# A decoder layer on one core: the weight products of its prologue chunk by chunk, and the first rows loaded beside them

## What is computed

```
x_norm = (x - mu) / sqrt(var + EPS) * gamma + beta
q = x_norm @ qkv[:, :KEY]
k = x_norm @ qkv[:, KEY:2 * KEY]
v = x_norm @ qkv[:, 2 * KEY:]
scores = einsum('bsk,btk->bst', q, k) * scale     # causal mask, softmax over t
out = attn @ v
out = out @ o_proj
return out + residual
```

## Time and profile before

| | |
|---|---|
| times of three runs | 1488.83, 1490.62, 1490.15 us; median 1490.15 |
| the profiled execution's own time | 1488.81 us |
| its span | 1487.0 us |
| TensorE busy | 1440.3 us, 97% of the span |
| VectorE, ScalarE, GpSimd busy | 71%, 44%, 39% |
| self-attention stage, from the trace | 0 to about 385 us |
| its prologue, until the bodies' first matmul | 0 to 40.99 us |

### The profile page before, as it was taken

One profiled execution on the slowest core, in us unless ns is written; L12 is line 12 of the kernel. 1 busy time (PEld: TensorE's weight loads), 2 busy tenths in 40 slices (PEclk: granted clock), 3 DMA queues, 4 the chain that ended last, 5 costly groups with the idle time before them and its releaser, 6 DMA issues. The chain is left out here.

```text
span 1487.0 us, 33650 instructions
## 1 busy us (share of the span) xinstructions
PE 1440.3 (97%) x13322; PEld 1123.5 (76%) x13322; DVE 1055.3 (71%) x2021; ACT 656.9 (44%) x865; POOL 579.2 (39%) x510
## 2 busy tenths in 40 slices
PE   7899999999899999999999999999999996899898
PEld 3688888887788888888888888888888885455343
DVE  2866565564477777877777778777787777677898
ACT  1333333333343343433433433334333332789996
POOL 0000000000144544555445545454545453753576
PEclk9999999999999999999999999999999998899999
DMA  6023333321511212112111121121111210439895
GB/s 219 29 79 103 103 103 102 102 76 52 184 41 42 73 45 72 39 45 72 45 47 64 45 72 39 45 72 45 56 55 45 72 46 24 107 113 327 274 348 200
DMA packets 80743, 138.59 MB, mean 93 GB/s; under 512 B 5218, under 2 KB 52834, under 8 KB 78898
## 3 DMA queue, kind: packets, MB, share of 16 engines
q1 hardware_dynamic: 80690, 137.87, 28.4%
HBM read 93.82 MB, written 44.04 MB: 93 GB/s over the span
## 5 line engine op out<-in xcount | busy, mean ns | idle before, releaser
L737 POOL TENSOR_TENSOR xa_psum<-xa_pr 125x448 f32<-125x448 f32 x126 | 153.9, 1221 | 236.3 <-DVE xa_pr L883 236.3
L883 DVE TENSOR_SCALAR xa_pr<-xa_pr,xa_keep 125x448 f32<-125x448 f32 x384 | 151.0, 450 | 108.3 <-ACT xa_pr L783 107.0
L783 ACT ACTIVATE xa_pr<-xa_bSC 125x1344 f32<-125x1344 f32 x128 | 165.6, 1293 | 138.3 <-PE xa_bSC L989 132.3
L764 ACT ACTIVATE xa_kf<-xa_bKV,xa_bk 128x376 f32<-128x376 f32 x128 | 73.6, 575 | 184.9 <-PE xa_bKV L913 184.9
L740 POOL TENSOR_TENSOR xa_psum<-xa_psum,xa_pr 125x448 f32<-125x448 f32 x126 | 147.0, 1167 | 12.1 <-POOL xa_psum L737 4.4
L913 PE MATMUL xa_bKV<-left_xn,wA 128*128 128x376 f32 x768 | 149.9, 344 | 0.0
L913 PE MATMUL xa_bKV<-xa_cx,wA 128*128 128x376 f32 x768 | 149.3, 343 | 0.0
L770 ACT COPY xa_v<-xa_bKV 125x512 f32<-125x512 f32 x96 | 56.2, 585 | 206.2 <-PE xa_bKV L924 201.1
L924 PE MATMUL xa_bKV<-wZ,left_xn 128*125 128x512 f32 x576 | 141.9, 394 | 1.7 <-POOL xa_ones L713 1.7
L924 PE MATMUL xa_bKV<-wZ,xa_cx 128*125 128x512 f32 x576 | 141.1, 393 | 0.0
L913 PEld LDWEIGHTS xa_bKV<-left_xn,wA 128*128 128x128 f32 x768 | 130.0, 188 | 8.9 <-issue 5.3
(11 more groups left out here) (193 smaller groups left out, 2508.8 us busy)
## 6 DMA issues: line engine op xcount, KB each, us to landing
wraw<-in_ctxT SPq DMA_DIRECT2D x32, 752.0 KB, 4.8
ff_hr<-h_scratch SPq DMA_DIRECT2D x28, 512.0 KB, 6.5
wraw<-in_w SPq DMA_DIRECT2D x8, 1024.0 KB, 7.7
sa_raw<-in_x SPq DMA_DIRECT2D x8, 896.0 KB, 5.9
x_scratch<-left_qraw SPq DMA_DIRECT2D x8, 896.0 KB, 5.1
xa_qf<-q_scratch SPq DMA_DIRECT2D x32, 224.0 KB, 4.9
xa_x<-x_scratch SPq DMA_DIRECT2D x32, 224.0 KB, 4.7
x_scratch<-xa_x SPq DMA_DIRECT2D x32, 224.0 KB, 2.3
```

The lines of the kernel that those rows point to most:

```text
L737: nc.gpsimd.tensor_tensor(psum01[:], third(h, 0), third(h, 1), ALU.add).then_inc(p01_ok, 1)
L783: nc.scalar.activation(pr[h][:], bSC[0:TW, :, 0:TC * S], ACT.Exp, scale=XSCALE).then_inc(exp_ok, 1)
L883: nc.vector.tensor_scalar(third(h, t), third(h, t), EM50, bound, ALU.max, ALU.min).then_inc(pr_ok, 1)
```

## The change

wqT and wkT are loaded chunk by chunk (eight loads of 256 KB, in pairs, each pair with a semaphore of its own). Products 0 to 3 are worked on together: for each chunk, the four matmuls into four different banks (`bM[0]`, `bM[1]`, `bS`, `bP`). So all four end in the last chunk. Products 4 to 7 go as before, into `bM[0]` and `bM[1]`, with `turned(0)` behind product 4 where it was ahead of product 7. Behind the eight loads SP loads the rows of group 0 into `x1`, which is the buffer `qraw`, and `statistics(0)` and `normalise(0)` read them there, ahead of every `product_low`. xwq, which needs the same buffer, is loaded once those rows are normalised. The rows of group 0 are loaded into `xt[0]` as well, as before, for the residual sum; VectorE waits for this load there.

```diff
+        bG = bM + [bS, bP] + bM + bM
-            for h in range(2):
+            for c in range(C):
                 for k, w in enumerate((wqT, wkT)):
-                    sp.dma_start(raw[k][:, 2 * h:2 * h + 2, :], w[:, 2 * h:2 * h + 2, :]).then_inc(w_in[h], 16)
+                    sp.dma_start(raw[k][:, c, :], w[:, c, :]).then_inc(w_in[c], 16)
+            sp.dma_start(x1, x_v[0]).then_inc(x0_in, 16)
             for k, w in enumerate((wvT, wo)):
-                sp.dma_start(raw[2 + k][:], w).then_inc(w_in[2 + k], 16)
+                sp.dma_start(raw[2 + k][:], w).then_inc(w_in[C + k], 16)
             for t, v in ((gam, gamma), (bet, beta), (bq, xbq)):
                 sp.dma_start(t[:], v).then_inc(small_in, 16)
-            sp.dma_start(qraw[:], xwq).then_inc(w_in[4], 16)
+            sp.wait_ge(xhat_ok, 4)
+            sp.dma_start(qraw[:], xwq).then_inc(w_in[C + 2], 16)
             sp.wait_ge(prod_done, 4)
...
-                nc.scalar.copy(w[0][:, k % 4, :], bM[k % 2][:, 0:D]).then_inc(prod_hi, 1)
-
-            for k in range(7):
-                product_high(k)
-            act.wait_ge(small_in, 48)
+                nc.scalar.copy(w[0][:, k % 4, :], bG[k][:, 0:D]).then_inc(prod_hi, 1)
...
+            for k in range(5):
+                product_high(k)
+            act.wait_ge(small_in, 48)
             turned(0)
-            product_high(7)
+            for k in range(5, 8):
+                product_high(k)
...
-                nc.vector.tensor_tensor(w[1][:, k % 4, :], bM[k % 2][:, 0:D], w[0][:, k % 4, :].bitcast(F32),
+                nc.vector.tensor_tensor(w[1][:, k % 4, :], bG[k][:, 0:D], w[0][:, k % 4, :].bitcast(F32),
...
             def statistics(g, par):
-                dve.wait_ge(x_in[par], 8 * (g - par) + 16)
+                rows = x1 if first(g) else xt[par]
+                if first(g):
+                    dve.wait_ge(x0_in, 16)
+                else:
+                    dve.wait_ge(x_in[par], 8 * (g - par) + 16)
...
                 dve.wait_ge(rh_ok, g + 1)
+                if first(g):
+                    dve.wait_ge(x_in[0], 16)
...
+            statistics(0, 0)
+            normalise(0, 0)
             for k in range(5):
                 product_low(k)
-            statistics(0, 0)
-            product_low(5)
-            normalise(0, 0)
-            product_low(6)
             split(0)
-            product_low(7)
-            dve.wait_ge(w_in[4], 16)
+            for k in range(5, 8):
+                product_low(k)
+            dve.wait_ge(w_in[C + 2], 16)
...
-            for k in range(8):
-                if k == 7:
+            for c in range(C):
+                pe.wait_ge(w_in[c], 32)
+                for k in range(4):
+                    mm = nc.tensor.matmul(bG[k][:, 0:D], raw[0][:, c, k * P:(k + 1) * P], raw[1][:, c, :], start=c == 0, stop=c == C - 1)
+                    if c == C - 1:
+                        mm.then_inc(prod_done, 1)
+            pe.wait_ge(w_in[C], 16)
+            pe.wait_ge(w_in[C + 1], 16)
+            for k in range(4, 8):
+                pe.wait_ge(prod_lo, k - 3 if k < 6 else k - 1)
+                for c in range(C):
+                    mm = nc.tensor.matmul(bG[k][:, 0:D], raw[2][:, c, (k - 4) * P:(k - 3) * P], raw[3][:, c, :], start=c == 0, stop=c == C - 1)
+                mm.then_inc(prod_done, 1)
+                if k == 4:
                     pe.wait_ge(const_ok, 2)
                     turned(0)
-                if k == 4:
-                    pe.wait_ge(w_in[2], 16)
-                    pe.wait_ge(w_in[3], 16)
-                a, b = (raw[0], raw[1]) if k < 4 else (raw[2], raw[3])
-                wait(pe, prod_lo, k - 1)
-                for c in range(C):
-                    if k == 0 and c % 2 == 0:
-                        pe.wait_ge(w_in[c // 2], 32)
-                    mm = nc.tensor.matmul(bM[k % 2][:, 0:D], a[:, c, (k % 4) * P:(k % 4 + 1) * P], b[:, c, :],
-                                          start=c == 0, stop=c == C - 1)
-                mm.then_inc(prod_done, 1)
```

More of the change, by code:

```diff
@@ L134, in self_attention @@
         bW = bP[:].bitcast(BF16)
+        bG = bM + [bS, bP] + bM + bM
         flat = wraw[:].rearrange("p c d -> p (c d)")
-        w_in, small_in = [n.sem(f"w_in{i}") for i in range(5)], n.sem("small_in")
-        x_in = [n.sem(f"x_in{p}") for p in range(2)]
+        w_in, small_in = [n.sem(f"w_in{i}") for i in range(C + 3)], n.sem("small_in")
+        x_in, x0_in = [n.sem(f"x_in{p}") for p in range(2)], n.sem("x0_in")
         zero_ok, const_ok = n.sem("zero_ok"), n.sem("const_ok")
@@ L331, in product_low @@
                 w = wA if k < 4 else wZ
-                nc.vector.tensor_tensor(w[1][:, k % 4, :], bM[k % 2][:, 0:D], w[0][:, k % 4, :].bitcast(F32),
+                nc.vector.tensor_tensor(w[1][:, k % 4, :], bG[k][:, 0:D], w[0][:, k % 4, :].bitcast(F32),
                                         ALU.subtract).then_inc(prod_lo, 1)
             def statistics(g, par):
-                dve.wait_ge(x_in[par], 8 * (g - par) + 16)
+                rows = x1 if first(g) else xt[par]
[3 more added lines that the diff above has]
+                    dve.wait_ge(x_in[par], 8 * (g - par) + 16)
                 for j in range(GB):
-                    nc.vector.bn_stats(st[:, j, :], xt[par][:, j, :]).then_inc(stat, 1)
+                    nc.vector.bn_stats(st[:, j, :], rows[:, j, :]).then_inc(stat, 1)
                 dve.wait_ge(stat, 8 * g + 4)
@@ L349, in normalise @@
                 for j in range(GB):
-                    nc.vector.tensor_scalar(xhat[:, j, :], xt[par][:, j, :], mv[:, j, 0:1], rstd[:, j:j + 1],
+                    nc.vector.tensor_scalar(xhat[:, j, :], rows[:, j, :], mv[:, j, 0:1], rstd[:, j:j + 1],
                                             ALU.subtract, ALU.mult).then_inc(xhat_ok, 1)
```

## The result

Six runs of the changed kernel have a median of 1485.2 us (1483.13 to 1486.42), six of the kernel before 1490.38 us (1487.04 to 1491.41). The ratio is 0.9968, 95% interval 0.9956 to 0.9981: faster by 0.3%, or 4.8 us, with 2.8 to 6.6 in the interval (the ratio is not the quotient of the medians, which lie 5.2 us apart). Forecast were 3.9 us less and a median of 1486.2. The profiled execution has a span of 1483.0 us where it had 1487.0.

A forecast was written before the change was run, and what follows sets the result against it. TensorE, busy for 97% of the span, was taken as the bound. A head start of 1.97 us plus 1.94 us of removed idleness gave 3.9 us, so 1490.15 - 3.9 = 1486.2 us, range 1484.3 to 1488.4.

The forecast's parts named there:

- The head start: First product matmul: starts at 4.8 instead of 6.77 us as smaller chunks land sooner, 1.97 us won, bounds 2.6 and 0.
- rival A: First loads: wkT's first chunk straggles, leaving a head start of 0 to 0.9 us, time 1487.4 to 1488.2; chance 0.16.
- The idle stretch: TensorE ahead of the transposes: the wait for normalised rows goes because x is loaded early, 1.94 us won.
- The failed step: Product 4's bank: product_low(0) done near 20.2, wanted at 21.4, cover 1.2 us even with VectorE held to 19.1.
- The sum: End of product 7: 36.8 us instead of 40.73, from 1.97 and 1.94 us won, gain 3.9 us.
- The clock at the start: First products: low clock costs 2.85 us, taken as unchanged; its length could shift the gain either way.
- rival B: First products: the clock rises no sooner than before, gain only 2.9 us, time 1487.2; chance 0.08.
- Is it kept?: Behind product 7: VectorE's chain to sa_wint moves by the same 3.9 us and later stages follow, so the gain stays.
- C: Second weight pair: product 4 waits for wo; slower by over 0.2% if it lands from 28.3 us on; chance 0.04.
- D: Whole kernel: nothing measurable, as something later absorbs the gain or the four banks cost it, 1489 to 1490; chance 0.05.

The follow-up runs named there:

- x_early_only: The kernel before with only group 0's rows loaded and normalised early, transposes behind product 4, weight halves and two banks kept: 1486.65 us, ratio 0.9981.
- again: The changed kernel itself, unaltered, measured and profiled once more: 1485.48 us, ratio 0.9974 to the kernel before.
- warm: The changed kernel with two extra fp32 matmuls on a tile of ones ahead of the wait for the first chunks: 1486.5 us, ratio 0.9981.
- x_behind: The changed kernel with the load of the first rows moved behind wvT and wo: 1492.29 us, ratio 1.0014.
- unit_first: The changed kernel with the first feed-forward block's quantisation, unit(0, 0, 0), ahead of the split of xwq on VectorE: 1485.98 us, ratio 0.9975.

## Why the prediction came out as it did, point by point

**The head start** was 2.27 us where 1.97 were taken. wkT's first chunk landed at 1.18 + 3.3 = 4.48; the straggling of rival A did not come. The Trainium skill (DMA: Bandwidth & Descriptors, "Anatomy of one DMA") gives its sum, about 2.0 us plus the bytes at 436 GB/s, for loads issued by GpSimd, and these are issued by SyncE. An estimate by it was 4.4; for this first pair, with nothing ahead of it in the queues, the trace agrees. For x, ninth in the queue, the same estimate is 4.1 us from issue to landing, and the trace has 10.2.

**The idle stretch** (1.94 us) went, as worked out; x_early_only alone measured 1.84.

**The failed step** is "VectorE is held by the statistics up to 19.1 at the latest, so this holds even there": the rows were normalised at 21.00. Both of its inputs were too small.

The first is the landing of x, 13.5 us at the latest; it was 14.7. The rate was not at fault. At 3.00 us 0.34 MB had been moved, and up to 13.6 us the changed kernel's queues had moved this much:

```profile
DMA packets 1662, 3.40 MB, mean 250 GB/s; under 512 B 143, under 2 KB 143, under 8 KB 1615
```

That is 3.06 MB in 10.6 us, 289 GB/s, as the sum had it. But the sum took it that the queues move first what was issued first. The eight chunks and x have 8 x 128 + 4 x 112 = 1472 rows of 2 KB; the packets from 2 KB to under 8 KB are 1615 - 143 = 1472 here, while at 13.3 us they are 1469, so the last row of x was moved between the two (the last chunk had landed at 4.01 + 7.2 = 11.2). By then 1662 - 1615 = 47 packets of 8 KB, 0.39 MB of the loads issued behind x, had been moved too. At that rate they take 1.3 us, about what x is late by.

The second is the chain from the landing to the normalised rows. The sum took 35.42 - 29.11 - 0.7 = 5.6 us, the 0.7 for the one `product_low` in between. It takes 21.00 - 14.73 = 6.27 us without that `product_low`, as long as it took with it before (35.42 - 29.15), because there the `product_low` ran while VectorE had to wait for GpSimd's power anyway:

```profile
32.26 0.68 DVE L332 TENSOR_TENSOR wZ<-sa_bM,wZ 128x512 fp32r<-128x512 f32 x1
...
32.43 1.03 POOL L229 TENSOR_TENSOR sa_rstd<-sa_ve,sa_half 112x4 f32<-112x4 f32 x1 [29.57 <-DVE sa_ve L344]
```

The wait for that power is 0.56 us before and 1.15 in the changed kernel. One error alone would have been covered. An estimate from these rows: with x at 14.73 and a chain of 5.6 us, `product_low(0)` is done by 21.1, just before product 4's turn at 21.18; with x at 13.5 and 6.27 us, by 20.5.

Since `product_low(0)` stands behind the whole normalisation, product 4 can start 7.01 us behind the landing of x at the earliest. It starts just then in all four profiles in which it waits for `product_low(0)`: 14.73 and 21.74 (changed), 14.66 and 21.68 (again), 15.10 and 22.11 (warm), 19.20 and 26.21 (x_behind). In the seven profiles in which x stands ninth it landed between 13.74 and 15.10 us; at 14.17 (unit_first) product 4 did not wait. So in both profiles of the changed kernel the end of the prologue hangs on one load of 0.9 MB and VectorE's chain behind it, not on TensorE's matmuls from the first chunk on. The sum added a head start on a path that no longer was the longest. The loss was small, 21.74 less 21.18 (product 3's end without its tail): 0.56 us.

**The sum** then reads 2.27 + 1.94 - 0.56 = 3.65; 0.12 us more was lost to the low clock (2.97 against 2.85), and 0.06 is left to the measured 3.47. Forecast were 3.9. That the two lie so close is in part luck: a head start 0.3 longer than taken made up for half of what the wait cost.

**The clock at the start.** The loss stayed at 21.18 - 4.50 - 32 x 0.4285 = 2.97 us, against 2.85 before, so rival B did not come; warm shows that the stretch follows the first work (its loss is 19.48 - 4.56 - 13.71 = 1.21). It differs between executions: 2.33 in the changed kernel's second profile, 2.6 to 2.3 in the three further profiles of the kernel before. What the Trainium skill says there (TensorE: Matmul & The Clock Gate, Part 1), that the number of slow matmuls at the start differs from run to run, this case's traces bear out.

**Is it kept?** Yes, but the clock plays over it. The lead at the landmarks of the two first profiles is 3.46 at L541, 2.4 at the start of the cross-attention (385.47 and 383.04 for its first load), 3.8 in the feed-forward part (1377.36 and 1373.57), 4.0 at the end. The loss of 1.0 comes in group 0, where the products of the attention weights with v follow an idle stretch of 1.9 us: before they ran at the full clock, in the profile after the clock was down:

```profile
67.89 5.43 PE L601 MATMUL sa_bO<-sa_raw,sa_pT 112*112 112x512 f32 x8 [1.90 <-ACT sa_pT L312]
...
69.00:70.00 1.00, 1.00 (x2) 0.31 (x1) 0.87 (x2) 0.00 (x0) 0.00 (x0) 0.50 0.00 0
```

The changed kernel's second profile has no fall there (its products are two rows of 1.97 and 1.94), and its first load of the cross-attention is issued at 381.96, so the whole lead, 3.51, has been kept up to there. Two of the further profiles of the kernel before have the fall (rows of 5.68 and 5.57). It is scatter and not the change. Of the 1.4 us won back in the feed-forward part, 1.05 appear at its second group of transposes (1281.07 and 1277.62), where TensorE waits 1.81 us for GpSimd before and 0.57 in the changed kernel; in the latter's second profile it waits 1.99 there, and the lead has shrunk to 1.64 when the first has 3.8, and is 2.8 at the end. So this is scatter too; its cause was not followed up.

**The measured 4.8 us** against 3.5 in the trace: the prediction had nothing for the runs in which the idle stretch also brings the clock down. The mean of L541 over four profiles of the kernel before is 51.53, over two of the changed one 47.76, a difference of 3.8, inside the interval. The second measurement of the changed kernel gives 0.9974, or 3.9 us. More than that the scatter does not allow; whether all of the remaining 1 us of the first is chance stays open.

**Rivals.** C, the late wo, did not come: it landed at 19.5, later than the 18.4 given as the latest, 1.7 us ahead of need. But its kin, a late x holding product 4 by way of VectorE, was the real danger: x_behind is slower than the kernel before with it. D did not come: the landmarks and both measurements show the gain.

## What to carry to other kernels

When work is moved ahead on an in-order engine, add up the path through every instruction that now stands behind it, and place the small one that frees a buffer ahead of the long one that nobody waits for yet. A head start at the front is worth only what the longest path leaves of it: in warm 1.7 us were won at the start and all of it was lost at the next wait, until that one was taken away too. A small piece of work that ran inside a wait for another engine saves nothing when it is moved away, so it must not be subtracted from the chain around it. And a load is not in when the bytes up to it have been moved: in the changed kernel 0.39 MB issued behind x went ahead of its last rows. An idle stretch of about 2 us on TensorE may cost more than its length.

## What was unexpected of the hardware

The clock column of the profile says 1.00 in the first 10 us although the matmuls run at half rate there (weight loads 0.85 us apart up to 10 us, 0.43 afterwards); the spacing has to be read. The granted clock fell after idle stretches of 1.9 to 2.2 us in some executions and not in others of the same kernel, and 1.8 to 2.2 us of idleness ahead of the transposes left it up in three of four profiles of the kernel before. Changing the PSUM bank with every fp32 matmul costs nothing: the weight loads of the changed kernel keep the same 0.43 us, bank after bank:

```profile
13.02 0.19 PEld L609 LDWEIGHTS sa_bP<-sa_raw 128*128 128x128 f32 x1 [0.24 <-issue]
13.45 0.19 PEld L609 LDWEIGHTS sa_bP<-sa_raw 128*128 128x128 f32 x1 [0.24 <-issue]
13.88 0.19 PEld L609 LDWEIGHTS sa_bM<-sa_raw 128*128 128x128 f32 x1 [0.24 <-issue]
```
